# One chain of eight attention groups, first weights loaded as two more experts, and the chosen experts' gates looked up inside the first round of experts

## The reference

```python
x = L0_attn_x                       # (2, 1024, 512) f32
xn = layernorm(x)
# attention: 16 heads in 4 groups, one key and one value head of 128 per group, causal
q, k, v = split_heads(xn @ w_q), split_heads(xn @ w_kv)
probs = softmax(where(causal, q @ k.T * 128**-0.5, -inf))
attn = (probs @ v).reshape(b, s, 2048) @ w_dense
# experts: 32, hidden 256; each token takes 6, out of the best 4 of 8 groups of experts
s = sigmoid(xn @ Wr.T + br)
idx = top_k(where(best_groups, s, 0), 6)
gate = 2.5 * s[idx] / (s[idx].sum() + 1e-20)
moe = sum(gate_e * (square(relu(xn @ W1[e].T)) @ W2[e].T) for e in idx)
shared = square(relu(xn @ Ws1.T)) @ Ws2.T
out = x + attn + moe + shared
```

## Time and profile before

| | |
|---|---|
| median of 3 runs | 1680.87 us (1679.23 to 1681.04) |
| the profiled execution, whole | 1680.17 us |
| its span, first to last instruction | 1677.9 us |
| PE busy | 1571.7 us (94%) |
| DVE busy | 1151.8 us (69%) |
| ACT busy | 858.1 us (51%) |
| mean granted PE clock | 0.976 of full |

### The profile page before, as it was taken

One profiled execution on the slowest core, in us unless ns is written; L12 is line 12 of the kernel. 1 busy time (PEld: TensorE's weight loads), 2 busy tenths in 40 slices (PEclk: granted clock), 3 DMA queues, 4 the chain that ended last, 5 costly groups with the idle time before them and its releaser, 6 DMA issues.

```text
span 1677.9 us, 31729 instructions
## 1 busy us (share of the span) xinstructions
PE 1571.7 (94%) x8812; PEld 1341.6 (80%) x8813; DVE 1151.8 (69%) x2335; ACT 858.1 (51%) x1767; POOL 292.9 (17%) x542
## 2 busy tenths in 40 slices
PE   6898899999999969999999999986999999999996
PEld 5776788888888857888888888865788888888885
DVE  6587665565565627857957957862795885885885
ACT  4454566666666624544545545532553453454453
POOL 0002333333333301011011011020100101101101
PEclk9899899999999989999999999997999999999999
DMA  5391666766676631012012012122111201201102
GB/s 203 131 407 40 201 215 210 240 214 222 216 229 218 210 103 45 20 57 63 19 56 63 19 56 82 39 90 100 45 32 45 63 23 52 63 21 54 39 7 82
DMA packets 61734, 180.14 MB, mean 107 GB/s; under 512 B 6736, under 2 KB 6864, under 8 KB 56912
## 3 DMA queue, kind: packets, MB, share of 16 engines
q1 hardware_dynamic: 36800, 107.84, 18.4%
q0 software_dynamic: 16640, 54.54, 11.7%
q10 hardware_dynamic: 8208, 16.78, 2.6%
HBM read 122.77 MB, written 56.36 MB: 107 GB/s over the span
## 4 chain that ended last, share of the span: by engine, by line
PE 89%; DVE 4%; issue 2%; ACT 2%; DMA 1%; DVEq 0%; ACTq 0%; POOLq 0%; SPq 0%
PE bank L595 8%; PE bank L597 8%; PE bank L596 8%; PE bank L885 7%; PE ps_s L595 6%; PE ps_s L597 6%; PE ps_s L596 6%; PE ps_s L873 5%; PE ps_s L874 4%; PE ps_s L868 4%; PE ps_s L766 4%; PE ps_s L770 3%; PE ps_s L767 3%; PE ps_s L781 3%; PE ps_s L785 3%; PE ps_s L782 3%
## 5 line engine op out<-in xcount | busy, mean ns | idle before, releaser
L1192 ACT ACTIVATE probs<-ps_s,negmax 128x128 f32<-128x128 f32 (+7 forms) x256 | 189.6, 741 | 177.8 <-DVE negmax L1573 176.8
L1222 DVE TENSOR_TENSOR pT_lo<-bank,pT_hi 128x512 fp32r<-128x512 f32 x288 | 196.3, 686 | 76.5 <-ACT pT_hi L1200 75.1
L1200 ACT ACTIVATE pT_hi<-bank 128x512 fp32r<-128x512 f32 x288 | 168.9, 596 | 149.9 <-PE bank L885 148.3
L1573 DVE TENSOR_REDUCE negmax<-ps_s 128x1 f32<-128x128 f32 (+7 forms) x256 | 188.9, 749 | 11.4 <-PE ps_s L874 8.9
L397 POOL TENSOR_TENSOR settled<-ident 128x1 f32<-128x1 f32 x192 | 54.3, 283 | 769.7 <-DVE acc L1600 760.1
L595 PE MATMUL ps_s<-xT_hi,wa_hi 128*128 128x512 f32 x384 | 156.5, 408 | 26.3 <-DVE wa_lo L1222 26.3
L885 PE MATMUL bank<-ident,probs 128*128 128x128 f32 x1152 | 167.8, 273 | 2.0 <-DVE pT_lo L1222 2.0
L885 PEld LDWEIGHTS bank<-ident,probs 128*128 128x128 f32 x1152 | 139.6, 141 | 29.7 <-DVE pT_lo L1222 2.4
L597 PE MATMUL ps_s<-xT_hi,wa_lo 128*128 128x512 f32 x384 | 153.1, 399 | 0.0
L596 PE MATMUL ps_s<-xT_lo,wa_hi 128*128 128x512 f32 x384 | 152.7, 398 | 0.0
L868 PE MATMUL ps_s<-kT_hi,qT_hi 128*128 128x512 f32 (+3 forms) x384 | 138.6, 361 | 6.1 <-ACT probs L1192 3.3
(11 more groups left out here) (190 smaller groups left out, 3695.4 us busy)
## 6 DMA issues: line engine op xcount, KB each, us to landing
eraw<-we SPq DMA_DIRECT2D x37, 1024.0 KB, 6.3
expert_outputs<-ysb SPq DMA_DIRECT2D x111, 256.0 KB
araw<-wa SPq DMA_DIRECT2D x40, 512.0 KB, 4.2
expert_outputs<-comb ACTq DMA_DIRECT2D x1, 16384.0 KB, 49.8
normed_tokens<-xn SPq DMA_DIRECT2D x4, 1024.0 KB, 6.3
out<-acc SPq DMA_DIRECT2D x2, 2048.0 KB, 8.2
res<-x SPq DMA_DIRECT2D x2, 1024.0 KB, 6.6
acc<-x SPq DMA_DIRECT2D x2, 1024.0 KB, 14.1
```

Source lines behind the costliest of these rows:

```text
L1192: act.activation(probs[:, i % 2, a, 0:keys], src, ACT.Exp, bias=negmax[:, i % 2, a:a + 1], accum_out=rowsum[:, i % 2, a:a + 1]).then_inc(e ...
L1200: act.activation(pT_hi[:, blk % RING, :], ps_t[blk % 2][:, :], ACT.Copy).then_inc(pt_hi_ready, 1)
L1222: dve.tensor_tensor(out_, whole, upper.bitcast(F32), ALU.subtract).then_inc(signal, 1)
L1573: dve.tensor_reduce(negmax[:, i % 2, a:a + 1], src, AX.X, ALU.max, negate=True).then_inc(max_ready, 1)
```

## The change

1. **Gates.** `find_gates` is cut into three functions (`match_rows`, `match_gates`, `sum_gates`), one 128x1536 instruction each. They run on DVE in experts 0, 1 and 2, two in each, under `If(es == 0)`. ACT no longer waits for the gates; what they read moves from `xn` to `xf01`.
2. **Slots.** The third and fourth slot of expert weights lie in `wa_hi`/`wa_lo`; expert 0 begins in slot 2 (`slot_of`). The two dummy experts behind the last now hold the first 4096 columns of attention group 0's weights, so they are split in place of W0 to W2; `FIRST` begins with K0. PE no longer waits for `room_free`; ACT does, behind `FIRST`.
3. **Bounds.** An expert's end is read two experts ahead, behind `hidden_tile(lo)` on PE and behind `upper_hidden`/`lower_hidden` on ACT and DVE, and carried over rounds in registers. PE's four `If`s become a tree of two levels.
4. **One chain.** `FIRST`, seven `GROUP`s and one `LAST` for both batches. Batch 1's `xT` is stored to `turned_tokens` in the shared stage (4 MB) and loaded in the fourth `GROUP`. `acc` is stored and z loaded tile by tile (256 KB each) in that `GROUP`; the last batch is stored tile by tile.

```diff
-        def over_experts(eng, body, row=0):
...
+        def over_experts(eng, body):
+            lo_reg = eng.alloc_register()
+            hi_reg = eng.alloc_register()
+            eng.reg_mov(lo_reg, 0)
+            eng.reg_mov(hi_reg, pair_bound(eng, 1))
             with eng.Fori(0, E // SLOTS) as es:
-                lo = pair_bound(eng, es * SLOTS, row)
+                lo = eng.snap(lo_reg, min_val=0, max_val=MAXT)
+                hi = eng.snap(hi_reg, min_val=0, max_val=MAXT)
                 for s in range(SLOTS):
-                    hi = pair_bound(eng, es * SLOTS + s + 1, row)
-                    body(es * SLOTS + s, s, lo, hi, es)
-                    lo = hi
-        def attend_groups(eng, attend, turn):
-            attend(FIRST, turn * GROUPS)
-            with eng.Fori(0, GROUPS - 1) as g:
-                attend(GROUP, turn * GROUPS + g, g)
-            attend(LAST, turn * GROUPS + (GROUPS - 1), GROUPS - 1)
+                    lo, hi = hi, body(es * SLOTS + s, s, lo, hi, es)
+                eng.reg_mov(lo_reg, lo)
+                eng.reg_mov(hi_reg, hi)
...
+        def attend_groups(eng, attend):
+            with eng.Fori(0, GROUPS_ALL - 1) as n:
+                attend(GROUP, n)
+            attend(LAST, GROUPS_ALL - 1)
...
+                if s == 0:
+                    for c in range(2):
+                        sp.wait_ge(xlo_ready, (c + 1) * HALF)
+                        for i, part in enumerate((xT_hi, xT_lo)):
+                            sp.dma_start(xT_d[c, i, :, :].rearrange("p (k n) -> p k n", k=KD),
+                                         part[:, :, c * C:(c + 1) * C].bitcast(F32)).then_inc(xT_out[c], 16)
```

```diff
+            def store_tile(b, t):
+                sp.wait_ge(dense_added, past(((b + 1) * GROUPS - 1) * NT + t + 1))
+                if t == 0:
+                    sp.wait_ge(comb_added, past(((b + 1) * GROUPS - 1) * NCOMB))
+                if t == NT - NT // GROUPS:
+                    sp.wait_ge(comb_added, past((b + 1) * GROUPS * NCOMB))
+                if b < B - 1:
+                    sp.wait_ge(out_done, past(t * 16))
+                sp.dma_start(outb[:, b * NT + t, :], acc[:, t, :]).then_inc(out_done, 16)
+            def load_z(t):
+                sp.wait_ge(out_done, past((t + 1) * 16))
+                sp.wait_ge(z_ok, past(GROUPS * (16 * NT) + t * 16))
+                sp.dma_start(acc[:, t, :], z_d[t * P:(t + 1) * P, :]).then_inc(z_ok, 16)
...
+            def switch_tiles(lo, hi):
+                for t in range(lo, hi):
+                    if t:
+                        sp.wait_ge(dense_added, past((GROUPS - 1) * NT + t + 1))
+                        load_z(t - 1)
+                    store_tile(0, t)
...
+            with sp.Fori(0, GROUPS_ALL - 1) as n:
+                load_piece(n + 1, 0)
+                load_piece(n + 1, 1)
+                with sp.If(n == GROUPS - 1):
+                    sp.wait_ge(z_out, 16)
+                    for c in range(2):
+                        sp.wait_ge(xT_out[c], 32)
                     sp.wait_ge(proj_ready, GROUPS * PROJ)
...
+                    for c in range(2):
+                        for i, part in enumerate((xT_hi, xT_lo)):
+                            sp.dma_start(part[:, :, c * C:(c + 1) * C].bitcast(F32),
+                                         xT_d[c, i, :, :].rearrange("p (k n) -> p k n", k=KD)).then_inc(xT_ok, 16)
+                    switch_tiles(0, 2)
+                with sp.Else():
+                    sp.sem_inc(xT_ok, 64)
+                    sp.sem_inc(z_ok, 16 * NT)
+                load_piece(n + 1, 2)
+                with sp.If(n == GROUPS - 1):
+                    switch_tiles(2, 4)
+                load_piece(n + 1, 3)
+                load_piece(n + 1, 4)
+                with sp.If(n == GROUPS - 1):
+                    switch_tiles(4, NT)
+                    load_z(NT - 1)
+                    sp.wait_ge(xT_ok, past((GROUPS + 1) * 64))
+                    sp.wait_ge(z_ok, past((GROUPS + 1) * (16 * NT)))
+            for t in range(NT):
+                store_tile(B - 1, t)
+            sp.wait_ge(out_done, past(16 * NT * B))
```

```diff
-                for slot in range(XG):
-                    with pe.If((p + 1) % XG == slot):
-                        transpose_gathered(slot, p + 1)
+                q = p + 1
+                with pe.If(q // 2 % 2 == 0):
+                    with pe.If(q % 2 == 0):
+                        transpose_gathered(0, q)
+                    with pe.Else():
+                        transpose_gathered(1, q)
...
-                hidden_tile(lo, s)
+                hidden_tile(lo, slot_of(s))
+                after = pair_bound(pe, e + 2)
...
-                    output_tile(lo - 1, s - 1)
+                    output_tile(lo - 1, slot_of(s - 1))
                 else:
                     with pe.If(es > 0):
-                        output_tile(lo - 1, SLOTS - 1)
...
+                            pe.wait_ge(xT_ok, past((n + 1) * 64))
+                        if isinstance(n, int) and n == 0 and j == 1:
+                            pe.wait_ge(y_copied, last + 1)
...
-            pe.wait_ge(room_free, 2)
-            with pe.Fori(0, B) as turn:
-                with pe.If(turn == 1):
...
-                    pe.wait_ge(xr_lo, NT)
-                attend_groups(pe, attend_pe, turn)
+            pe.wait_ge(ew_lo, (NSH + E + 1) * WP + 2)
+            pe.wait_ge(mx_lo, last + 1)
+            attend_pe(FIRST, 0)
+            attend_groups(pe, attend_pe)
```

```diff
+            act.wait_ge(z_out, 16)
             for c in range(2):
-                upper_weights(c, 0, NSH // 2 + 1)
-            for h in range(2):
-                act.wait_ge(xn_out[h], 16 * B)
+                upper_weights(c, slot_of(0), NSH // 2 + 1)
+            for c in range(2, WP):
+                upper_weights(c, slot_of(0), NSH // 2 + 1)
             upper_tokens(0)
-            act.wait_ge(y_ready, OUTS)
-            act.wait_ge(z_out, 16)
-            act.wait_ge(gates_ready, B)
-            for c in range(2, WP):
-                upper_weights(c, 0, NSH // 2 + 1)
             for c in range(WP):
-                upper_weights(c, 1, NSH // 2 + 1)
+                upper_weights(c, slot_of(1), NSH // 2 + 1)
...
-            add_output(3, 0)
-            find_gates(0)
-            add_output(3, 1)
-            find_gates(1)
-            add_output(3, 2)
...
+            add_output(3, 0)
+            lower_weights(0, 0, slot_of(0))
+            lower_weights(0, 1, slot_of(0))
+            add_output(3, 1)
+            lower_weights(0, 2, slot_of(0))
+            lower_weights(0, 3, slot_of(0))
+            add_output(3, 2)
             lower_tokens(0)
             add_output(3, 3)
-            dve.wait_ge(z_out, 16)
-            for c in range(2, WP):
-                lower_weights(0, c, 0)
             for c in range(WP):
-                lower_weights(1, c, 1)
+                lower_weights(1, c, slot_of(1))
...
                 square_hidden(lo)
                 lower_tokens(lo + 1)
                 lower_weights(e + 2, 0, slot)
                 lower_hidden(lo)
+                after = pair_bound(dve, e + 2)
                 lower_weights(e + 2, 1, slot)
+                if s == 0:
+                    with dve.If(es == 0):
+                        match_rows(0)
+                elif s == 1:
+                    with dve.If(es == 0):
+                        sum_gates(0)
+                elif s == 2:
+                    with dve.If(es == 0):
+                        match_gates(1)
                 with dve.Fori(lo + 1, hi) as p:
                     square_hidden(p)
                     lower_tokens(p + 1)
                     lower_hidden(p)
                 lower_weights(e + 2, 2, slot)
                 lower_weights(e + 2, 3, slot)
+                if s == 0:
+                    with dve.If(es == 0):
+                        match_gates(0)
+                elif s == 1:
+                    with dve.If(es == 0):
+                        match_rows(1)
+                elif s == 2:
+                    with dve.If(es == 0):
+                        sum_gates(1)
+                return after
```

```diff
+    first = wa[:P, :2 * W_COLS].reshape(P, 2, W_COLS).transpose(1, 0, 2)
+    we = np.ascontiguousarray(np.concatenate([we[:E], first, we[:AHEAD - 2], we[E:]], axis=0).reshape((E + AHEAD + NSH) * P, W_COLS))
```

More of the change, by code:

```diff
@@ L1141, in expert_uppers @@
                 upper_hidden(lo)
+                after = pair_bound(act, e + 2)
                 upper_weights(1, slot, arrived)
@@ L1205, in attend_act @@
                         act.activation(cT_hi[:, :], ps_ctx[:, :], ACT.Copy).then_inc(ctx_hi_ready, 1)
[L1207 to L1214 removed]
+            for e in range(2):
+                act.wait_ge(eraw_in[e], ALL_IN[e])
+            attend_act(FIRST, 0)
+            act.wait_ge(room_free, 1)
+            attend_groups(act, attend_act)
         @block.vector
@@ L1540, in expert_lowers, with attend_dve @@
```

(16 more changed lines are left out.)

216 lines of the change are left out of this document (93 added, 123 removed).

## The result

The changed kernel takes 1605.57 us, median of 4 runs (1604.21 to 1606.8), before 1680.95 (1679.23 to 1682.16, 4 runs): ratio 0.9552 with a 95% interval of 0.9536 to 0.9569. The forecast was 1611.0 with a range of 1600 to 1627. The profiled execution took 1606.8 us with a span of 1604.9; before's were 1680.17 and 1677.9.

The account below looks back on a forecast made before the run. PE bounds the attention groups, so gains come only from places PE does not fill: -6.6 + 5.2 - 11.0 - 15.1 - 36.6 - 5.8 = -69.9, giving 1610.3 us, 1611.0 as a median, range 1600 to 1627.

Parts of the forecast that it names:

- Experts to attention: Last expert tile to first projection and the stretch behind: minus 13.0 and minus 2.1, together minus 15.1 us.
- change of batch: Between the two turns of attention groups: one chain makes four equal periods, 506.3 us instead of 542.88, minus 36.6.
- end: Behind the last addition: only the eighth tile's 256 KB store remains instead of one 2 MB store, minus 5.8 us.
- The rival of a collision: At the change of batch, stores and loads all queue behind the eighth addition: plus 20, 1631 us; chance 0.07.
- Before the experts, -6.6: Up to the third expert tile: without six gate instructions ahead, PE reaches it at 176.5 against 183.07 us.
- the shared stage: zero: The 4 MB of xT stores on SP in the shared stage cost nothing; a bound of plus 2 us.
- The other five gate instructions, +5.2: In the experts' tiles: DVE's slack hides part of five 1.75 us instructions, plus 5.2 us; bounds 0 and 8.8.
- Bounds in registers, -11.0: Expert boundaries: round tops and boundaries save 16.3 us, loads amid tiles cost 5.3; bounds minus 16.3 and plus 7.
- The +5.3 for loads amid the tile: In 31 experts, the bound's load between turned tile and output product costs 0.17 us each, plus 5.3.
- The register loads only move: Rival at the expert boundaries: PE waits behind the moved loads instead, minus 11.0 becomes 0, 1622 us; chance 0.24.
- All hidden: Rival in the experts: loads and gates hidden, -16.3 and +1 replace -11.0 and +5.2, 1601.5 us; chance 0.12.
- The sequencer: Slower rival in all 111 expert tiles: the tree of Ifs makes PE's sequencer the bound, 1694 us at 0.75; chance 0.02.

Follow-up runs that it names:

- the kernel in which all engines read: Changed kernel with expert bounds read as before, at a round's top and ahead of every expert, on all four engines: 1628.63 us, ratio 0.9699.
- the four kernels above: Changed kernel with expert bounds read at the boundary again: by PE 1617.96 us, by DVE 1626.01, by DVE, ACT and SP 1628.11, by all 1628.63.
- the one with the gates in `FIRST`: Changed kernel with its six gate instructions at full length moved behind the experts into FIRST: 1593.63 us, ratio 0.9487.
- the one with the short gate instructions: Changed kernel with its six gate instructions cut in place from 1536 elements to 32 and 48: 1595.3 us, ratio 0.9496.

## Why the prediction came out right, point by point

- **Experts to attention, change of batch, end.** Met: -13.0 and -2.2 for -15.1; -36.5 for -36.6; -5.7 for -5.8. Each rested on a distance between two rows of one mark and a store or wait with a measured duration. The store's part of the first is now shown by an experiment, the end's too, and the cover of the xT loads (61 us for 14.4). The stores and z loads keep up: DVE's eighth addition starts at 1115.30, the last tile of z has landed at 1122.26, and the next group's first addition comes at 1132.50, so the forecast's 7 of 17 us were right too. The rival of a collision is out. Of the three weight pieces only one was loaded in the gap.
- **Before the experts, -6.6.** The mechanism was right and the size measured from the stage's own end too: from the last lower unit of the shared stage to the third tile it was 30.1 us and is 23.4, 6.7 less. What failed is "the shared stage: zero". It came 3.0 later in this execution and 1.1 to 3.1 in all profiles, and not because of the stores. Also wrong was the picture within the term: PE was to run at 2.4 GHz, and it waits 1.67 us at tile 0 and falls to 1.2.
- **The other five gate instructions, +5.2.** The step that failed is "DVE has some 1.0 us of slack in pieces". They cost 11.5 us (12.1 less the 0.6 without them), over the upper bound of 8.8. Slack in pieces is no slack for an instruction of 1.75 us. The three behind two weight pieces, taken at 0.75 each, made PE wait 1.78 to 1.89 us and their steps 2.22 to 2.25 longer. The two behind a single piece, taken at 1.5, stand in steps 1.95 and 1.82 longer, the first of them with the clock down for most of it. And the bound of 5 x 1.75 held the work only: it left out 0.3 us until the dependent instruction starts, and the clock. Behind the waits at 191.76 and 227.81 PE's granted clock was 0.50 for 3.4 us each time; the last long step, 5.06 us with no gate instruction in it, is that alone.
- **Bounds in registers, -11.0.** The runs give -24.7 for the kernel, beyond the bound of -16.3. The +5.3 for loads amid the tile was right: in the changed kernel 27 of the 94 steps hold one, most of them take 3.62 us, and together they are 4.2 over, 0.16 each where the forecast took 0.17. What failed is the price of the old boundaries, and that the sum counted PE's reading alone. The forecast took 0.30 for an ordinary boundary, from a step of 3.78, which is among the shortest: the 21 such steps before are 0.52 over at the mean. It left out the step behind the boundary: 246.43 has the next one 4.22 later, at 250.65, with PE waiting for DVE, and the 67 steps without a load before are 5.2 us over in all, 0.9 after. And of the 0.28 us that were to stay at the top of a round some 0.07 are left. The same place in the kernel before has DVE's price too, 0.64 us ahead of its square with nothing but its sequencer to wait for:

  ```profile
  249.69 0.43 DVE L1507 TENSOR_TENSOR mhsq<-mrelu 128x256 f32<-128x256 f32 x1 [0.64 <-issue]
  ```

  ```profile
  250.17 0.44 PE L794 MATMUL ps_s<-ident,mhsq 128*128 128x128 f32 x2 [0.23 <-DVE mhsq L1507]
  ```

  The median of a load on PE, 0.31 us, was measured rightly and isn't the price: DVE stood still for 0.64 us to read one bound and for 1.37 to read two.
  The Trainium skill, "DMA: Bandwidth & Descriptors", section "Latency and other measured facts", has about 600 ns as the floor of a `tensor_load`. The changed kernel's median on PE is 302 ns (34 loads), on ACT 278, so it doesn't hold as a floor here.
- **The sum.** -12.0 for the experts was forecast as -5.8: an error of +6.3 in the gates (+11.5) and of -12.5 in the registers (-23.5, which is what is left; the kernel in which all engines read gives 22.9 for the same steps). With the +3.0 of the shared stage the sum came within 3.1 us of the profile. That is luck in part: the two errors have opposite signs by chance, not by a common cause.
- **The rivals.** "The register loads only move" is refuted by the four kernels above. "All hidden" was nearest on the boundaries, though low (-16.3), and had the gates wrong. The sequencer isn't the bound of a tile: the steps are 3.48 as before, and of the 67 without a load between tiles 16 and 110 none is over 3.59. The Trainium skill, "Runtime: NRT & Kernel Launch", section "Instruction fetch mechanics", lets a taken branch out of the fetched window stall; in none of these steps is there such a stall.

## What to carry to other kernels

When several engines do the same small thing at the same place (read a bound, pass a branch), price it on each of them; the profile shows only the latest, and the others' share appears when that one is gone. The gain is then near the maximum of them (24.7 here, with 12.8 for PE's reading alone and 19.5 for DVE's), and changing only the engine that the profile names gained 1.7. And where an instruction is put into the gaps of another engine's loop, ask whether one gap takes it whole: the same 10.5 us of DVE work cost some 11 us in the experts' tiles and nothing in a stretch where DVE had 4.7 us of work in 24.5.

## What the runs showed of the hardware

The same idle time doesn't always bring the clock down. The changed kernel and the one with the gates in `FIRST` have the same two waits of PE at the start of the first group (1.41 and 1.63 us; 1.41 and 1.64), and the 5 us behind, busy throughout in both, differ:

```profile
610.00:615.00 5.00, 5.00 (x24) 4.17 (x23) 3.46 (x6) 2.74 (x4) 2.09 (x2) 0.83 0.17 45
```

```profile
596.40:601.40 5.00, 5.00 (x28) 4.24 (x27) 4.78 (x10) 3.18 (x6) 2.09 (x2) 1.00 0.21 56
```

The first period is 128.0 us in the one and 126.4 in the other; of the thirteen profiles of changed kernels seven have the one and six the other. It is a step of 1.6 us, and single executions of one kernel lie 4 us apart and more: the one with the short gate instructions took 1593.4 twice and 1597.1 twice. A difference of 2 us between two profiles is no finding until the clock of the stretches has been compared.
